# A chunked delta-rule recurrence: sums of means and variances and two batches' state on TensorE, k and v projected from steps 10 and 9, running products two at a time

## The reference, cut to what matters

```
q = silu(conv4(x @ Wq.T));  k = silu(conv4(x @ Wk.T)) / 8;  v = silu(conv4(x @ Wv.T))
a = sigmoid(x @ Wa.T + ba); beta = sigmoid(x @ Wb.T + bb)
def step(S, (qt, kt, vt, at, bt)):            # per batch and head, S is 64 values x 64 keys
    err = S @ kt - vt
    S   = at[:, None] * S - bt * (err[:, None] * kt[None, :])
    o   = S @ qt
mu, var = o.mean(-1), ((o - mu)**2).mean(-1)  # over the 64 values of a head
o = (o - mu) / sqrt(var + 1e-5) * ln_w + ln_b
x = x + (o * sigmoid(x @ Wg.T)) @ Wo.T
```

## Time and profile before

| | us |
|---|---|
| median of 3 runs | 4142.81 (4140.54 to 4145.77) |
| profiled execution, its own time | 4146.99 |
| its span, first to last instruction | 4145.2 |

### The profile page before, as it was taken

One profiled execution on the slowest core, in us unless ns is written; L12 is line 12 of the kernel. 1 busy time (PEld: TensorE's weight loads), 2 busy tenths in 40 slices (PEclk: granted clock), 3 DMA queues, 4 the chain that ended last, 5 costly groups with the idle time before them and its releaser, 6 DMA issues. The chain is left out here.

```text
span 4145.2 us, 108628 instructions
## 1 busy us (share of the span) xinstructions
PE 3221.6 (78%) x44353; PEld 2229.0 (54%) x44353; DVE 3377.1 (81%) x6152; ACT 1856.4 (45%) x4394; POOL 2488.9 (60%) x2981
## 2 busy tenths in 40 slices
PE   6677777777777777777777774377999979998998
PEld 4354554554554554554554553354666647755775
DVE  4999999999999999998999998206888868856885
ACT  4232332332332332332332331225888879937982
POOL 0777777777777777877877776332010058806870
PEclk9787777777777777777777876588999989998999
DMA  2111111111111111101101100410000011201110
GB/s 76 40 34 29 42 33 33 38 32 35 38 31 37 36 31 35 39 30 37 33 27 36 35 25 24 132 38 20 2 2 2 2 31 38 44 6 36 41 37 26
DMA packets 156241, 138.91 MB, mean 34 GB/s; under 512 B 65351, under 2 KB 108579, under 8 KB 155487
## 3 DMA queue, kind: packets, MB, share of 16 engines
q1 hardware_dynamic: 153438, 129.25, 11.5%
q0 software_dynamic: 2304, 2.71, 0.2%
HBM read 96.12 MB, written 16.82 MB: 27 GB/s over the span
## 5 line engine op out<-in xcount | busy, mean ns | idle before, releaser
L1105 DVE TENSOR_TENSOR a_tmp<-a_h,banks 128x128 f32<-128x128 f32 (+14 forms) x960 | 723.2, 753 | 96.7 <-POOL a_h L870 39.5
L1111 DVE TENSOR_REDUCE a_h<-a_tmp 128x64 f32<-128x128 f32 (+14 forms) x960 | 723.0, 753 | 26.4
L870 POOL TENSOR_TENSOR a_h<-a_h,a_a 128x128 f32<-128x128 f32 (+11 forms) x768 | 586.2, 763 | 182.0 <-DVE a_h L1111 162.6
L707 ACT ACTIVATE a_va<-banks 128x512 f32<-128x512 f32 x128 | 136.9, 1069 | 737.1 <-PE banks L544 737.1
L855 POOL TENSOR_TENSOR a_st<-a_st,a_ab 128x512 f32<-128x512 f32 x256 | 327.2, 1278 | 0.0
L889 POOL TENSOR_TENSOR a_p<-a_p,a_dk 128x384 f32<-128x384 f32 x64 | 92.7, 1449 | 353.8 <-DVE a_h L1090 353.8
L544 PE MATMUL banks<-a_w_v,a_xseg 128*32 128x512 f32 x2048 | 297.6, 734 | 0.0
L539 PE MATMUL banks<-a_bias_v,k_ones_row 1*128 1x512 f32 x128 | 101.1, 880 | 233.7 <-DVE a_h L1111 233.3
L530 PE MATMUL banks<-a_xseg,a_w_k 128*128 128x128 f32 x2048 | 244.5, 280 | 40.4 <-DVE a_h L1111 34.7
L1956 ACT ACTIVATE c_s<-c_s,c_low 128x384 f32<-128x384 f32 (+1 forms) x512 | 266.5, 580 | 18.9 <-DVE c_low L1900 13.6
L530 PE MATMUL banks<-a_xseg,a_w_q 128*128 128x128 f32 x2048 | 271.8, 299 | 0.0
(11 more groups left out here) (296 smaller groups left out, 8121.1 us busy)
## 6 DMA issues: line engine op xcount, KB each, us to landing
a_ab<-decays SPq DMA_DIRECT2D x512, 128.0 KB, 3.0
d_Vs<-d_V SPq DMA_DIRECT2D x128, 128.0 KB, 2.4
sent<-k_nothing SPq DMA_DIRECT2D x40, 64.5 KB, 2.3
b_xe<-sent SPq DMA_DIRECT2D x8, 322.5 KB, 3.6
a_xseg<-xn SPq DMA_DIRECT2D x32, 70.0 KB, 3.2
xn<-a_xnT SPq DMA_DIRECT2D x8, 256.0 KB, 2.7
a_xrow<-in_L_attn_x SPq DMA_DIRECT2D x128, 16.0 KB
x<-a_xrow SPq DMA_DIRECT2D x128, 16.0 KB, 1.9
```

The costliest lines, as they stand in the source:

```text
L870: e.tensor_tensor(self.history(ch, t + 1)[:, :, 0:t], self.history(ch, t)[:, :, 0:t], at, ALU.mult).then_inc(*self.s_hist.at((g, t)))
L1105: e.tensor_tensor(prod, both, gram, ALU.mult).then_inc(*step.at((g, t, "product")))
L1111: e.tensor_reduce(self.results(ch, t), prod, AX.X, ALU.add).then_inc(*step.at((g, t, "w")))
```

## The change

Means and variances: `pe_moment` now sums all of `o2` (or of its squares, `o1`) over the partitions of a head and over eight groups of four rows, with eight matmuls that add up in one bank; VectorE reduces the 128 columns that are left (`dve_moment`), behind step 4 of each chunk. `dve_total` and `dve_spread` go, and `act_moment` with them; the square root is `act_root`.

State: for batches 0 and 1 the decayed state is put into U's banks by a matmul with the identity (`pe_carry`), `pe_U` adds to it there, and ScalarE copies the sum back (`act_state`). VectorE keeps the additions for batches 2 and 3.

Order: `LATE` becomes `HOLD`, 10 for k and 9 for v. `pe_out` moves from chunk 0 to chunk 1, the mean's matmuls ahead of the time rows. GpSimd makes the running products in twos between the history products of chunk 1, centres in halves, gates at the end of chunk 0 and adds the rows of x at the end of the segment. SP issues the decay DMAs ahead of the row stores. The Gram rows of VectorE move into chunk 1 behind step 14.

Layout: `dc` and `dk` have the position innermost. ScalarE writes the Gram matrices once, with four quarter activations over the first chunk's partitions, and VectorE's transpose reads each head twice; `pool_gram` goes. `og` holds both halves.

```diff
-LATE = 12
+HOLD = {"k": 10, "v": 9}
-            self.a2, self.bv, self.dc = two("a2_", [P, 32, SEG]), sb("bv", [P, 32, SEG]), two("dc", [P, SEG, 32])
-            self.dk = sb("dk", [P, CK, 32])
+            self.a2, self.bv, self.dc = two("a2_", [P, 32, SEG]), sb("bv", [P, 32, SEG]), two("dc", [P, 32, SEG])
+            self.dk, self.last = sb("dk", [P, 32, CK]), two("last", [P, NCK, 32])
...
     def take(self, q, key):
-            q.wait_ge(self.s_evac, self.ring[n - 2])
+            last = self.ring[n - 2]
+            q.wait_ge(self.s_moment if last[0] in ("mean", "dev") else self.s_evac, last)
...
     def pe_moment(self, e, q, s, which):
         b = self.take(q, (which, s))
-        q.wait_ge(self.s_tot, (which, s))
-        e.matmul(b[:, 0:SEG], self.cst["row_mean"][:], self.tot[:], start=True, stop=True).then_inc(*self.s_full.at((which, s)))
+        if which == "mean":
+            q.wait_ge(self.s_o, 2 * s + 1)
+        else:
+            q.wait_ge(self.s_squared, s)
+        of = self.o2[s % 2] if which == "mean" else self.o1
+        for m in range(8):
+            t = e.matmul(b[:, 0:P], self.cst["row_mean"][:], of[:, 4 * m:4 * m + 4, :].rearrange("p i t -> p (i t)"),
+                         start=(m == 0), stop=(m == 7))
+        t.then_inc(*self.s_full.at((which, s)))
...
     def pe_P(self, e, q, s, ch):
-                q.wait_ge(self.s_st, (g - 1, pair + 1))
+                q.wait_ge(self.s_st if pair else self.s_state, (g - 1, pair + 1))
...
+    def pe_carry(self, e, q, g):
+        for n in range(2):
+            if g:
+                q.wait_ge(self.s_state, (g - 1, n))
+            else:
+                q.wait_ge(self.s_zeroed, 1)
+            q.wait_ge(self.s_decay, (g, n))
+            e.matmul(self.ubank(n), self.c.ident[:], self.ST[:, 8 * n:8 * n + 8, :].rearrange("p r v -> p (r v)"),
+                     start=True, stop=False).then_inc(*self.s_carried.at((g, n)))
...
     def tensor(self, e, q):
             self.pe_P(e, q, s, 0)
+            if old >= 0:
+                self.pe_moment(e, q, old, "mean")
...
-            if old >= 0:
-                self.pe_moment(e, q, old, "mean")
...
-            if older >= 0:
-                self.pe_out(e, q, older)
-            if more:
-                q.wait_ge(self.s_step, (g, LATE, "w"))
+                q.wait_ge(self.s_step, (g, HOLD["k"], "w"))
                 for half in range(2):
                     self.pe_project(e, q, "k", nxt, half)
+            self.pe_carry(e, q, g)
             self.pe_U(e, q, s, 0)
...
-                q.wait_ge(self.s_step, (g, LATE, "w"))
+            if older >= 0:
+                self.pe_out(e, q, older)
+            if more:
+                q.wait_ge(self.s_step, (g, HOLD["v"], "w"))
                 for half in range(2):
                     self.pe_project_rows(e, q, "v", nxt, half)
+            self.pe_carry(e, q, g)
             self.pe_U(e, q, s, 1)
...
     def act_gram(self, e, q, s, par):
-        e.activation(self.Gb[:, :, :, heads].rearrange("p z t r -> p r z t"), v[:, 0], ACT.Copy, scale=half_of[:, 0:1])
-        e.activation(self.Ga[:, :, :, heads].rearrange("p z t r -> p r z t"), v[:, 1], ACT.Copy,
-                     scale=half_of[:, 1:2]).then_inc(*self.s_evac.at(("gram", s, par)))
+        e.activation(dst, v[:, 1], ACT.Copy, scale=-1 / 8).then_inc(*self.s_gwhole.at((s, par)))
+        q.wait_ge(self.s_gwhole, (s, par))
+        for bi in range(NB):
+            rows = slice(bi * SEG, bi * SEG + CK)
+            t = e.activation(dst[rows], v[rows, 0], ACT.Copy, scale=-1 / 8)
+        t.then_inc(*self.s_evac.at(("gram", s, par)))
...
+    def act_state(self, e, q, g):
+        for n in range(2):
+            q.wait_ge(self.s_u, (g, 1))
+            e.activation(self.ST[:, 8 * n:8 * n + 8, :].rearrange("p r v -> p (r v)"), self.ubank(n),
+                         ACT.Copy).then_inc(*self.s_state.at((g, n)))
...
     def gpsimd(self, e, q):                      # chunk 1
             self.pool_rest(e, q, s, 1)
-            self.pool_history(e, q, s, 1, HAND, 7)
+            for t in range(HAND, 12):
+                self.pool_history(e, q, s, 1, t, t + 1)
+                if more:
+                    self.pool_cumulate(e, q, nxt, 2 * (t - HAND), 2 * (t - HAND) + 2)
             self.pool_query(e, q, s, 1)
...
             if more:
-                self.pool_cumulate(e, q, nxt)
                 self.pool_prepare(e, q, nxt, 0)
+                self.pool_gram_rows(e, q, nxt)
             if old >= 0:
                 self.pool_scale(e, q, old)
             if more:
                 self.pool_values(e, q, nxt)
-                self.pool_gram_rows(e, q, nxt)
+            if older >= 0:
+                self.pool_add(e, q, older)
...
+    def dve_moment(self, e, q, s, which):
+        q.wait_ge(self.s_full, (which, s))
...
+        e.tensor_reduce((self.mom if which == "mean" else self.var)[:], self.held((which, s))[:, 0:P].rearrange("p (i t) -> p t i", t=SEG),
+                        AX.X, ALU.add).then_inc(*self.s_moment.at((which, s)))
...
     def dve_steps(self, e, q, s, ch):
-            if ch == 1 and t == 13 and s:
+            if t == HAND and s:
+                self.dve_moment(e, q, s - 1, "dev" if ch else "mean")
+            if ch == 1 and t == 10 and s:
                 self.dve_reciprocal(e, q, s - 1)
+            if ch == 1 and t == 14 and s + 1 < self.nseg:
+                self.dve_gram_rows(e, q, s + 1)
...
     def dve_state(self, e, q, s, ch):
-        for n in range(4):
+        for n in range(2, 4):
             sv = self.ST[:, 8 * n:8 * n + 8, :].rearrange("p r i -> p (r i)")
```

More of the change, by code:

```diff
@@ L627, in pe_U @@
                         t = e.matmul(self.ubank(bi)[par * DK:(par + 1) * DK, ct * DK:(ct + 1) * DK], self.Kt[rows, k0:k0 + DK],
-                                     self.Wt[rows, x:x + 2, :].rearrange("p h i -> p (h i)"), start=True, stop=True)
+                                     self.Wt[rows, x:x + 2, :].rearrange("p h i -> p (h i)"), start=(pair > 0),
+                                     stop=(pair > 0 or ct == NCT - 1))
             t.then_inc(*self.s_u.at((g, pair + 1)))
@@ L811, in scalar @@
                     self.act_gate(e, q, older, n)
-            if old >= 0:
-                self.act_moment(e, q, old, "mean")
             if more:
@@ L823, in scalar @@
                     self.act_project(e, q, "k", nxt, half)
+            self.act_state(e, q, g)
             self.act_gram_bank(e, q, g + 1)
             self.act_gate_rows(e, q, g + 1)
+            if more:
+                self.act_project(e, q, "q", nxt, 0)
             if old >= 0:
-                self.act_moment(e, q, old, "dev")
+                self.act_root(e, q, old)
+            if more:
+                self.act_project(e, q, "q", nxt, 1)
+                for n in range(2):
+                    self.act_gram(e, q, nxt, n)
+            if older >= 0:
+                self.act_out(e, q, older)
             if more:
                 for half in range(2):
-                    self.act_project(e, q, "q", nxt, half)
-                for n in range(2):
-                    self.act_gram(e, q, nxt, n)
-                for half in range(2):
                     self.act_project_rows(e, q, "v", nxt, half)
+            self.act_state(e, q, g + 1)
+            if more:
                 self.act_gram_bank(e, q, g + 2)
@@ L967, in gpsimd @@
     def gpsimd(self, e, q):
-        self.pool_cumulate(e, q, 0)
+        self.pool_cumulate(e, q, 0, 0, CK)
         self.pool_prepare(e, q, 0, 0)
-        for n in range(2):
-            self.pool_gram(e, q, 0, n)
         self.pool_gram_rows(e, q, 0)
```

182 lines of the change are left out of this document (78 added, 104 removed).

## The result

The changed kernel takes 4028.43 us (median of 4 runs, 4018.29 to 4031.51) against 4144.29 (4140.54 to 4151.74) for the kernel before: ratio 0.9714, 95% interval 0.9691 to 0.9737, so 2.9% faster. The forecast was 3985, its range 3885 to 4100. The profiled execution took 4030.5 us, its span is 4028.7. Of the 116.5 us that the span lost, 112.6 lie between the first and the last transpose of W; the start-up gives 2.5 and what follows the recurrence 1.4.

What follows compares the result with a forecast made beforehand. VectorE was taken to set the pace, TensorE right behind it. A segment of 72.3 us against 77.4 gave 31 x 5.1 = 158, with 3 more 161, off 4147: 3986, stated as 3985; range 3885 to 4100.

Steps and rivals of the forecast that it cites:

- the steps: VectorE's sixteen steps in each half of a segment: 26.2 us in A (from 26.9), 27.8 in B (from 27.0).
- the crossing after B: From half B's last step to the next transpose of P: 1.8 + 7.65 us, where it was 14.8.
- The rival with the running products at double price: GpSimd's running products cost twice as much in the new order: 77.3 us a segment, no change, 4140; chance 0.07.
- the port wait: After B, GpSimd's scaling of o holds up VectorE's o2 subtraction at the SBUF port: up to 2.0 us.
- Out before it raises the clock, as it does for k in all segments now, so v costs 4.7 + 4.7: TensorE in B: v runs at the high clock behind out, ending at 28.7 us from P's end.
- The crossing after A: From half A's last step to the next transpose of P: 1.8 + 4.7 us, plus 1.9 of late TensorE on average.
- the low way: TensorE in A with a at the low clock, 7.9 us, and k 9.69: done at 34.7, late by 5.5.
- The prediction's W: End of W's transpose on VectorE, counted from P's end: 29.2 us in A, 29.7 in B.
- the high way: TensorE in A at the high clock: a 4.2, k 7.4, carry 1.8, done at 28.7; two segments of three.
- the rival of a slower kernel: TensorE's clock low at a, k, v's first half and both crossings: 79.4 us a segment, 4209; chance 0.08.
- The carries: Two matmuls a chunk on TensorE putting decayed state into U's banks: 1.8 us, charged only where TensorE is late.
- v near 19.3: In half B, TensorE starts projecting v near 19.3 us, counted from P's end, after Gram and out.

Runs made afterwards that it cites:

- e1: The change plus eight unread 128x128 matmuls on TensorE between the Gram matrices and the output projection of chunk 1: 3968.45 us.
- e10: The change with unread matmuls before out, all four state additions on VectorE (no carry), and GpSimd's scaling of o behind VectorE's second o2 subtraction: 3941.83 us.
- e11: e10 plus eight more unread matmuls ahead of U in chunk 0 and eight between U and P: 3938.45 us.
- e8: The change with unread matmuls before out in chunk 1 and no carry, VectorE adding all four state parts: 3967.07 us.
- e4: The change with the state part undone: no carry, VectorE adds U to all four batches' state, ScalarE copies nothing back: 3986.74 us.
- e9: The change with k and v held until step 12 instead of 10 and 9: 4027.55 us.
- e6: The change with the output projection, its gate products and ScalarE's part back in chunk 0, between a and k: 4167.25 us.
- e5: The change with one wait added: GpSimd starts scaling o only after VectorE's second o2 subtraction has ended: 4006.2 us.

## Why the prediction was right, and where it was off

The time fell inside the range and on the forecast's side, by the mechanism it named for the steps and crossings: VectorE has less to do in them. What bounds the crossing after B it had wrong. Its sum was 72.3 us a segment; 73.9 came.

- **The steps.** 26.2 and 27.8 were forecast, 26.2 and 27.3 measured. The reductions out of the bank cost 0.28 (0.3 taken), dk's product over 384 elements 1.02 instead of 1.45 (0.95 forecast), the one over 512 1.30 (1.3 forecast), and the waits for GpSimd fell from 69.1 to 4.6 us. The rival with the running products at double price fell: 413 ns each, where 377 was before and 360 was looked for, and nobody waits for them.
- **The crossing after B is the step that failed in size.** It was put at 9.45 (1.8 + 7.65), bound by the port wait, with TensorE late by 0.9 behind it. It is 11.48, bound by TensorE, late by 3.89. The sentence at fault is "Out before it raises the clock, as it does for k in all segments now, so v costs 4.7 + 4.7". Out started behind a gap, 2.43 us in the segment shown (70.2 us in 30 segments, L599), in which TensorE waits for ScalarE's Gram quarters, and itself ran at the low level, 3.78 us; v's first half after it took 2.07 + 6.51 instead of 1.12 + 3.64, 3.8 us more, in 25 of the 29 segments that have an out. Before, out stood directly behind 7 us of a, nearly all low too, and k behind it was high; the sentence carried that over to a place with a gap. e1 shows it: work put into the gap gives 60 us, and 31 x 2.03 = 63 is what the term was short of. In three of the other four segments the level came back while out ran, as the sentence wanted (segment 2: out, then v's first bias pair):

```profile
296.88 3.42 PE L599 MATMUL banks<-a_w_o,a_y 128*128 128x128 f32 x16 [2.43 <-ACT a_g L745]
300.24 1.12 PE L539 MATMUL banks<-a_bias_v,k_ones_row 1*128 1x512 f32 x2
```

- **The port wait** was sized at 2.0 and is 1.2: 1.92 us for a subtraction of 0.69. The scaling starts 0.25 us behind W (mean of 29 crossings), where W + 1.05 was worked out, so it holds the subtraction for less of it. The traces agree with the rule of the Trainium skill (SBUF — State Buffer, "Who interferes with whom") that the instruction issued first keeps the port: in the change the subtraction ends 0.55 us behind the scaling that started before it, and in e10, ahead of the scaling, it takes 0.69. In the change it costs nearly nothing, as TensorE is later still; e10 shows it at full price. VectorE's bound with it is 8.6 where 9.45 was worked out.
- **The crossing after A** was put at 6.5 plus 1.9 of lateness, 8.4; it is 8.87. The lateness is 1.29 on average and comes in the two ways named (0.12 to 0.6, and 2.3 to 3.8), and TensorE is over 2 us late in 13 of 30 segments, where one in three was forecast. In these k took 9.0 to 9.5 us (9.69 was taken), but a was mostly low in its second half alone (14 of 62 bias pairs in all), so the low way costs 2.3 to 3.8 and not 5.5. The prediction's W is off too: by its own terms it comes at 0.1 + 26.2 + 1.8 = 28.1 behind P's end and not at 29.2, so that the high way, 28.7, is 0.6 late and not in time; 0.12 to 0.6 was measured. More late segments at a smaller price bring the average near the forecast, which is luck. What was missing: even with U in time the crossing is 7.0 to 8.9. In those of 8.7 TensorE stands idle some 2.3 us before U, and U and P then take 3.35 and 3.4 us, where 1.99 and 1.9 to 2.3 are seen at the high level (e11, e8); in those of 7.0 to 7.1 P takes 2.5. This was charged only in the rival of a slower kernel.
- **The carries** were rightly sized (1.8 taken, 1.99 measured) and "charged only where TensorE is late". That is every crossing after B (late by 0.99 at least) and 13 of 30 after A, so this edit loses 42 us (e4).
- **"HOLD of 10 for k (passed at 16) does not bind either"** came true: k waits 1.3 us for its step in one segment and nowhere else. A hold of 12 binds (0.66 us in the segment shown), and after A TensorE comes 1 us later; in time nothing changes (e9).
- **v near 19.3** came true (19.15), right behind out, which itself waits for the first Gram half's evacuation (e6). ScalarE's Gram quarters took 0.60 us each, where 0.5 to 0.71 was taken.
- **The sum again**, with measured terms: 26.22 + 8.87 + 27.32 + 11.48 = 73.9; against 72.3 that is 31 x 1.6 = 50, and 3985 + 50 = 4035, beside the 4028 measured. Of the 1.6, 2.0 come from B's crossing and 0.5 from A's, less 0.5 in B's steps and the 0.45 for issue gaps, which these crossings hold already.

What stays open: why the low level at v's first half is less frequent in e5 and e9 (22 and 12 pairs) than in the change (27), with v starting at the same place. In all three it is low only where out took 3.78 us or more; what brings the level back sooner, while out runs, isn't shown.

## What to carry to other kernels

When an edit takes work off the bounding engine, work out the second engine's arrival at each crossing at both clock levels, from the rows of both levels, and look at the gap ahead of the first of its instructions: a projection behind a gap is priced low until a row shows the contrary. Moving 1.2 us of additions to an engine that the others wait for cost more than it freed here. A port wait under a later arrival was nearly free until that arrival was mended, and then it was due in full: mend in the order in which the waits end.
